# One attentional factorization kernel: its head is rebuilt and the transposes of the next batch block move from round 6 to round 12

## The reference

```
V = emb_v[x]                                   # x: 32 x 2048 indices
VV = V[iu] * V[ju]                             # 496 pairs
hid = relu(einsum('pbk,kh->pbh', VV, at_w) + at_b)
score = einsum('pbh,ho->pbo', hid, at_h)
pooled = sum(VV * score, axis=0)
logit = pooled @ p + w0 + sum(w1[x], axis=0)
prob = sigmoid(logit)
```

## Time and profile before

| What | Value |
|---|---|
| median of 3 runs | 841.13 us |
| span of the profiled execution | 835.8 us |
| runs' median less the span | 5.3 us |
| PE busy | 784.1 us (94%) |
| DVE busy | 722.5 us (86%) |
| ACT busy | 640.7 us (77%) |
| POOL busy | 555.4 us (66%) |
| PE share of the chain that ended last | 86% |
| DMA queue q0 (the gathers) | 16896 packets, 17.07 MB |

### The profile page before, as it was taken

One profiled execution on the slowest core, in us unless ns is written; L12 is line 12 of the kernel. 1 busy time (PEld: TensorE's weight loads), 2 busy tenths in 40 slices (PEclk: granted clock), 3 DMA queues, 4 the chain that ended last, 5 costly groups with the idle time before them and its releaser, 6 DMA issues.

```text
span 835.8 us, 26345 instructions
## 1 busy us (share of the span) xinstructions
PE 784.1 (94%) x10550; PEld 277.6 (33%) x10550; DVE 722.5 (86%) x1221; ACT 640.7 (77%) x674; POOL 555.4 (66%) x537
## 2 busy tenths in 40 slices
PE   0488996999999999999999999999999999999998
PEld 0123332333333333333333333333333333333332
DVE  4278897699999999999999999999999999999894
ACT  0267775788798887878878788898888888888785
POOL 5577777666677676666766766677667666766720
PEclk9989998999999999999999999999999999999999
DMA  7533268445423466544332347644434457633200
GB/s 257 99 25 24 26 22 25 23 22 22 23 22 23 20 22 23 21 22 24 21 22 22 23 21 22 23 24 21 22 21 23 21 22 23 24 22 22 11 1 1
DMA packets 19398, 24.27 MB, mean 29 GB/s; under 512 B 9960, under 2 KB 10029, under 8 KB 19373
## 3 DMA queue, kind: packets, MB, share of 16 engines
q0 software_dynamic: 16896, 17.07, 43.4%
q1 hardware_dynamic: 1535, 6.64, 2.1%
q10 hardware_dynamic: 942, 0.22, 0.1%
HBM read 20.59 MB, written 3.31 MB: 29 GB/s over the span
## 4 chain that ended last, share of the span: by engine, by line
PE 86%; DMA 5%; POOL 5%; issue 2%; ACT 1%; DVE 0%; ACTq 0%; POOLq 0%
PE Z L591 52%; PE SG L607 26%; POOL rows L303 5%; PE SG L621 4%; PE Z L553 4%; DMA rows<-table,joint_idx 3%; DMA rows<-in_L_rec_emb_v_dram,idx 2%; ACT pV L471 0%; ACT H L526 0%; DMA idx_raw<-in_r_x_dram 0%; PE Z L685 0%; ACT V L460 0%; PE Z L664 0%; ACT y_sb L537 0%; ACTq L247 0%
## 5 line engine op out<-in xcount | busy, mean ns | idle before, releaser
L303 POOL DMA_INDIRECT rows<-table,joint_idx x496 | 518.8, 1046 | 224.0 <-issue 139.7
L445 DVE TENSOR_TENSOR X<-V 128x992 f32<-128x992 f32 (+15 forms) x1024 | 635.6, 692 | 28.8 <-ACT V L500 14.8
L526 ACT ACTIVATE H<-Z,bias 128x1024 f32<-128x1024 f32 x512 | 529.7, 1121 | 113.2 <-PE Z L591 109.8
L591 PE MATMUL Z<-X,w_sb 64*64 64x512 f32 x4096 | 477.2, 600 | 7.4 <-DVE X L445 3.4
L591 PEld LDWEIGHTS Z<-X,w_sb 64*64 64x64 f32 x4096 | 147.0, 132 | 288.7 <-issue 283.2
L607 PE MATMUL SG<-H,score_w 128*32 128x512 f32 x2048 | 239.4, 597 | 0.0
L607 PEld LDWEIGHTS SG<-H,score_w 128*32 128x32 f32 x2048 | 56.8, 109 | 172.8 <-issue 96.0
L471 ACT ACTIVATE pV<-V,pmask 128x1024 f32<-128x1024 f32 x64 | 81.5, 1276 | 0.1
L413 DVE TENSOR_TENSOR prod<-SG,gram 128x512 f32<-128x512 f32 x32 | 22.1, 691 | 63.3 <-PE SG L607 63.3
L460 ACT COPY V<-Z 128x1024 f32<-128x1024 f32 x31 | 31.4, 1013 | 42.4 <-PE Z L553 42.4
L621 PEld LDWEIGHTS SG<-V,pV 128*32 128x32 f32 x4096 | 42.7, 109 | 23.9 <-issue 19.3
(11 more groups left out here) (46 smaller groups left out, 35.1 us busy)
## 6 DMA issues: line engine op xcount, KB each, us to landing
rows<-table,joint_idx POOLq DMA_INDIRECT x496, 3.7
table<-joined SPq DMA_DIRECT2D x4, 792.0 KB
H<-in_L_rec_emb_v_dram SPq DMA_DIRECT2D x4, 768.0 KB, 8.3
rows<-in_L_rec_emb_v_dram,idx POOLq DMA_INDIRECT x16, 5.3
w_all<-in_L_rec_w_dram,idx POOLq DMA_INDIRECT x16
idx_raw<-in_r_x_dram SPq DMA_DIRECT2D x2, 64.0 KB, 2.1
idx_raw<-in_r_x_dram ACTq DMA_DIRECT2D x2, 64.0 KB, 2.3
table<-tail SPq DMA_DIRECT2D x1, 54.7 KB
```

Source lines behind the costliest of these rows:

```text
L303: pool.indirect_dma_start(out=rows[t % 2][:, g * FILL_M + m, half, c0:c1], out_offset=None, in_=source, in_offset=bass.IndirectOffsetOnAxi ...
L445: last_one = nc.vector.tensor_tensor(xo, vj, vi.unsqueeze(3).to_broadcast(shape), ALU.mult)
L526: nc.scalar.activation(H[:, s % H_SLOTS, :, COLS * g:COLS * g + COLS], Z[:, z_slot(t, r), :, :], ACT.Relu, bias=bias[:, 0:1]).then_inc(hid ...
L591: done = nc.tensor.matmul(Z[64 * par:64 * par + 64, z_slot(t, r), half, :], w_sb[k, :], X[k, s % X_SLOTS, par, COLS * g:COLS * g + COLS], ...
```

## The change

The head is written in another way, and the order within a fill changes:

- ACT makes the joined table in place of DVE, with the same eight copies.
- On ACT's queue the load of the tail of `w1` moves ahead of the weights; the loads of `bias`, `p`, `h` and `w0` move from ACT's to SP's queue, behind the loads of the table.
- Fills 0 and 1 are gathered from the given table; POOL's waits for the joined table stand ahead of fill 2. The separate `w1` gathers at the end become 32.
- The semaphores `rows_landed` and the waits on them are gone. The constant `IN_FLIGHT` is 4, and no line of the changed kernel reads it or `HELD_FILLS`.
- `V` of fill 0 is copied from PSUM by DVE in place of ACT, and the constants that need `p` and `h` are made by DVE behind round 1 of fill 0.
- The transposes for every fill from 2 on stand ahead of round 12, and the scaled copies on ACT ahead of rounds 14 and 15.
- The loop over fills starts at fill 1.

```diff
-TURN_BEFORE, LATE_TURN = 6, 12
-LATE_FILLS = (1, 2)
+TURN_BEFORE, SCALE_BEFORE = 12, (14, 15)
...
-PLAIN_FILLS = 1
+PLAIN_FILLS = 2
...
-LANES, IN_FLIGHT, HELD_FILLS = 4, 3, 4
+IN_FLIGHT, HELD_FILLS = 4, 4
...
             sp.dma_start(tail[:, :, 1:1 + EMB], last_rows(emb_v)).then_inc(tail_loaded, 16)
+            for half in range(2):
+                lo, hi = half * 64, half * 64 + 64
+                sp.dma_start(bias[lo:hi, :], at_b.rearrange("(h o) -> h o", o=1)).then_inc(bias_loaded, 16)
+                sp.dma_start(pcol[lo:hi, :], p).then_inc(p_loaded, 16)
+                sp.dma_start(hcol[lo:hi, :], at_h).then_inc(h_loaded, 16)
+            sp.dma_start(w0_sb[:, :], w0.to_broadcast([QUARTERS, 1])).then_inc(w0_loaded, 16)
...
-                            n = GATHERS * t + 2 * (FILL_M * g + m) + half
-                            if held and n >= IN_FLIGHT:
-                                pool.wait_ge(rows_landed[(n - IN_FLIGHT) % LANES], 16 * ((n - IN_FLIGHT) // LANES + 1))
...
             gather(0)
+            pool.wait_ge(idx_ready, 2)
+            gather(1)
             pool.wait_ge(idx_ready, 4)
             pool.wait_ge(table_stored, 16 * (PIECES + 1))
-            gather(1)
             pool.wait_ge(first_turned, 2)
             gather(2)
...
+            act.wait_ge(w1_loaded, 32)
+            for c in (0, 1 + EMB):
+                nc.scalar.copy(joined[:, :, c], raw_w1[:, :]).then_inc(w1_joined, 1)
+                nc.scalar.copy(tail[:, :, c], tail_w1[:, :]).then_inc(w1_joined, 1)
+            for k in range(PIECES):
+                act.wait_ge(raw_loaded[k], 16)
+                r0, r1 = k * PIECE, (k + 1) * PIECE
+                nc.scalar.copy(joined[:, r0:r1, 1:1 + EMB], raw[:, r0:r1, :]).then_inc(rows_joined[k], 1)
...
-                        late = turn_before(t) == LATE_TURN
-                        if r == turn_before(t):
+                        if r == TURN_BEFORE:
                             keep_v(t + 1, 1 - parity)
-                        if r == (14 if late else 12):
+                        if r == SCALE_BEFORE[0]:
                             keep_pv(t + 1, 1 - parity, 0)
                             keep_w1(t + 1, 1 - parity)
-                        if r == (15 if late else 14):
+                        if r == SCALE_BEFORE[1]:
                             keep_pv(t + 1, 1 - parity, 1)
...
-            products(1, 1, False, False)
-            products(2, 0, False, False)
-            products(3, 1, False, False, head)
-            with pe.Fori(3, FILLS - 2, 2) as t:
+            products(1, 1, False, False, head)
+            with pe.Fori(1, FILLS - 2, 2) as t:
```

More of the change, by code:

```diff
@@ L195, in afm_kernel @@
         w1_first = sem("w1_first")
-        rows_landed = [sem(f"rows_landed{lane}") for lane in range(LANES)]
+        first_gathered = [sem(f"first_gathered{g}") for g in range(2)]
         first_turned = sem("first_turned")
@@ L222, in over_fills @@
             fill(0, 0, True, False)
-            fill(1, 1, False, False)
-            fill(2, 0, False, False)
-            with eng.Fori(3, FILLS - 2, 2) as t:
+            with eng.Fori(1, FILLS - 2, 2) as t:
                 fill(t, 1, False, False)
@@ L230, in gathered @@
         def gathered(t, parity):
-            return 16 * GATHERS // 2 * (t - parity - HELD_FILLS + 2)
-        def landed(gathers):
-            return 16 * gathers // LANES
+            return 16 * GATHERS // 2 * (t - (1 if parity else 2) + 2)
         def piece(dram, k):
@@ L348, in _ @@
                                         ).then_inc(idx_ready, 1)
-            dve.wait_ge(w1_loaded, 32)
-            for c in (0, 1 + EMB):
-                nc.vector.tensor_copy(joined[:, :, c], raw_w1[:, :]).then_inc(w1_joined, 1)
-                nc.vector.tensor_copy(tail[:, :, c], tail_w1[:, :]).then_inc(w1_joined, 1)
-            for k in range(PIECES):
-                dve.wait_ge(raw_loaded[k], 16)
-                r0, r1 = k * PIECE, (k + 1) * PIECE
-                nc.vector.tensor_copy(joined[:, r0:r1, 1:1 + EMB], raw[:, r0:r1, :]).then_inc(rows_joined[k], 1)
             nc.vector.memset(score_w[:, :, :], 0.0).then_inc(score_w_cleared, 1)
@@ L426, in products @@
                     if first and r in (0, STEPS // 2):
+                        first_keep_v(g)
                         dve.wait_ge(first_v, g + 1)
+                    if first and r == 2:
+                        loaded_consts()
                     if r == 8:
@@ L542, in turn @@
             def turn(t, parity):
-                if isinstance(t, int) and t < HELD_FILLS:
-                    for lane in range(LANES):
-                        pe.wait_ge(rows_landed[lane], landed(GATHERS * (t + 1)))
-                    pe.nop(nofuse=True)
-                else:
-                    pe.wait_ge(rows_gathered[parity], gathered(t, parity))
+                pe.wait_ge(rows_gathered[parity], gathered(t, parity))
                 embs = rows[parity][:, :, :, :].rearrange("p t h k -> p t (h k)")
@@ L557, in first_turn @@
             def first_turn(g):
-                for lane in range(LANES):
-                    pe.wait_ge(rows_landed[lane], landed(GATHERS // 2 * (g + 1)))
-                pe.nop(nofuse=True)
+                pe.wait_ge(first_gathered[g], 16 * GATHERS // 2)
                 if g == 1:
@@ L580, in hidden @@
                 pe.wait_ge(x_ready, ROUNDS * t + r + 1)
-                if r == turn_before(t) + 2 and not first and not last:
+                if r == TURN_BEFORE + 2 and not first and not last:
                     pe.wait_ge(v_ready, t + 1)
                 elif not first or r >= Z_SLOTS:
-                    pe.wait_ge(hid_ready, ROUNDS * t + z_before(t, r) + 1)
+                    pe.wait_ge(hid_ready, ROUNDS * t + z_before(r) + 1)
                 pe.nop(nofuse=True)
@@ L634, in products @@
                 for r in rounds:
-                    if r == turn_before(t) and not first and not last:
-                        pe.wait_ge(hid_ready, ROUNDS * t + turn_before(t) - Z_SLOTS + 1)
+                    if r == TURN_BEFORE and not first and not last:
+                        pe.wait_ge(hid_ready, ROUNDS * t + TURN_BEFORE - Z_SLOTS + 1)
                         turn(t + 1, 1 - parity)
```

68 lines of the change are left out of this document (29 added, 39 removed).

## The result

| What | Before | After |
|---|---|---|
| median of 4 runs each | 839.81 us (837.4 to 841.59) | 852.0 us (850.7 to 852.45) |
| ratio after to before | | 1.0155, 95% interval 1.0118 to 1.0192 |
| span of the profiled execution | 835.8 us | 850.6 us |
| that execution's own time | 837.4 us | 852.45 us |

The account below looks back on a forecast made before the run. PE alone was taken to set the pace in the loop. The terms summed as 835.8 + 21.1 - 6.8 - 0.6 - 8.1 = 841.4 us of span, +5.3 = 846.7 us, with a range of 838 to 861.

Parts of the forecast that it names:

- the likeliest case: Whole kernel: the forecast of 846.7 us, slower, with its own range of 842.5 to 850 and chance 0.60.
- The wait in the loop: Fills 5 to 30: PE waits for ACT's `pV` ahead of the inner products; 24.93 us a fill, +21.1 us.
- The 0.66 us for long products: Inner products as long as in fill 2, left out of the loop; as a rival 17 us on top, chance 0.10.
- Fills 3 and 4: Late transposes find fill 4's rows there, so the 6.74 us stall goes: -6.8 us.
- The head, -8.1: Up to fill 1: 16th gather lands at 32 in place of 40.1, fill 1's transposes stand at 55.5; -8.1 us.
- Edits costed at nothing: Rest of the head, such as ACT's joins, DVE's constants and small loads on SP's queue: put at nothing.
- The constants on DVE: First half of fill 0: under 1.1 us, hidden by the wait for the second half of its gathers.
- ACT's joins: Head: four joins on ACT take about 6 us together against DVE's 3.55, put at no cost.
- The 32 `w1` gathers: End: 16 further gathers go out until about 821, PE wants them at about 830; no cost.
- The 5.3 us around the span: Whole kernel: runs' median lies 5.3 us above the span of 835.8, added to the predicted span.
- That of the port pair: Head: GpSimd can't write descriptors during DVE's join, so the 4.48 us gather's extra 3.5 us go with it.
- That of the turns, packet by packet: Head: a gather should lose little beside bulk traffic, second half of fill 0 at about 28; not followed.

Follow-up runs that it names:

- e1: Kernel before, old head kept, with the transposes of every fill ahead of round 12; 1182.36 us, ratio 1.037, on a slow chip.
- f2: Changed kernel with both scaled copies ahead of round 14, one relu fewer in ACT's chain; 846.48 us, ratio 1.0071 to the kernel before.
- f4: Kernel before, old head kept, with every fill's transposes ahead of round 12 and both scaled copies ahead of round 14; 847.48 us, ratio 1.0056.
- f1: Kernel before with the whole new head and its own order of rounds kept; 843.8 us, ratio 1.0014.
- f3: Changed kernel with gathers of fills 0 and 1 held to three in flight and small loads back on ACT's queue; 855.21 us, ratio 1.0152.
- g4: Changed kernel with the eight joining copies on DVE again; run once, 853.54 us, where the kernel before takes 837.65.

## Why the prediction was right, and where it was not

The direction, the mechanism and the range were right: 852.0 us lies in 838 to 861, though 2 us over the likeliest case's own 842.5 to 850. The size was not: 12.2 us slower against 5.6. By its steps:

*The wait in the loop.* Right. Predicted was a wait of about 0.6 us or more ended by `pV`, and a period of 24.93 us; the trace has 0.54 us in all 26 and 24.79. The size was 0.14 us a fill too large: I took ACT's chain at 6.7 + 0.18 us, and it is 6.75, with 1.27 us and not 1.30 for a scaled copy. From the transposes' start to the inner products it took 496.17 - 488.23 = 7.94 us where I had 8.03. Without the few fills whose products are long the periods are 24.79 and 24.10 us: 26 x 0.69 = 18.0 us, and three such fills in place of one make it 19.2. `e1`, `f2` and `f4` show the mechanism from both sides: the wait comes with the late order under the old head too, and goes with one relu. The 0.66 us for long products was left out of the loop for a reason that doesn't hold, so that it came out nearly right is luck. It is not a matter of straight code: fill 2 of before, with 2.10 us, has two gather issues of POOL that end during its products (those at 119.16 and 120.41), and the loop shows the same in `f2` and `f4`.

*Fills 3 and 4.* Right in kind, -8.1 where I had -6.8. What I left out stands in the windows of the kernel before:

```profile
134.00:136.00 2.00, 0.00 (x0) 0.00 (x0) 1.52 (x3) 0.00 (x0) 1.53 (x2) 0.50 0.81 22
136.00:138.00 2.00, 1.99 (x12) 1.66 (x16) 0.00 (x0) 0.00 (x0) 1.55 (x2) 0.50 0.91 28
138.00:140.00 2.00, 2.00 (x16) 0.74 (x20) 0.32 (x1) 1.26 (x2) 0.43 (x2) 0.71 0.76 22
```

The 6.74 us stall lowered the granted clock to 0.50, and the transposes and the six rounds behind it took 1.5 us more. A stall costs its own length and the slow stretch after it. The row was there to be read: 1.97 us for transposes that take 1.09 elsewhere.

*The head, -8.1.* This step failed; measured is +0.2. I let the 16th gather land at 32; it landed at 39. I had moved its issue forward, from 36 to 24.5 (it went out at 23.6), and added a landing time of another stretch of the trace. The landing time is what grew: 3.5 us with three in flight on free DMA engines, 15.4 with no hold beside the table's traffic. The changed head was bound by how fast gathers land and not by when they are issued; `f1` (ratio 1.0014), `f3` and `g4` show the second half within about 2 us of the same place in differently built heads. The first half did gain 6.7 us, which nothing could use.

*Edits costed at nothing.* The constants on DVE were hidden in the end, but with 5.4 us of waiting ahead of them: they stood behind small loads of which I had only asked whether they delay the stores. The stores waited for SP's blocked queue and shared the DMA engines with the gathers: the four pieces were stored by 58 us and the table's tail by 62, against 26 and 30 before, and fill 2's gathers began at 63.00 where I had them at 47.3. So fill 2's rows were late: 2.25 us of waiting at 88.67 and 1.6 us of slow clock behind it (the transposes 1.47 us instead of 1.09, the 32 matmuls after them 4.92 instead of 3.66). That is the +3.5 of fills 1 and 2. `f3` wins 3.4 us of it back in fill 1 and gives it up again before and behind.

*ACT's joins.* Right: 5.59 us, where I had 6. *The 32 `w1` gathers:* their cover held; no wait for them appears.

*The 5.3 us around the span.* Wrong. They compared a median with another execution's span. The execution that was profiled took 837.4 us, 1.6 above its span, and after it is 1.85. With 1.7 in their place my sum would have been 843.1, 8.9 us below the median, where 846.7 misses by 5.3; that the error of this term hid part of the others was luck. Between the spans the miss is 9.2 us: the head (8.3) and fills 1 and 2 (4.1), less the loop, which I had too dear (1.9), and fills 3 and 4, which gained more (1.3).

*The two rules.* That of the port pair: the trace agrees, and `g4` shows it by itself. That of the turns, packet by packet: my reading, that a gather loses little, was wrong (39 and not 28 us). In the changed kernel between 36 and 60 us:

```profile
q0 software_dynamic: 484, 0.48, 66.6%
q1 hardware_dynamic: 287, 1.50, 15.1%
```

Worked out over 16 engines and 24 us, a gather's packet takes 528 ns for 1 KB and a store's 202 ns for 5 KB. If the queues take turns by packet, the bulk transfer loses more than the gather. The rule itself (the Trainium skill, DMA: Bandwidth & Descriptors, section "Queues, rings and completion order") may hold; no run here tests it, and `g4`, whose four pieces were stored by 38 us with no hold, shows that more than turns decides.

*What stays open.* How a gather issue on POOL and a long block of 128 short matmuls on PE hang together, though they always come together; why the stores of the table end 20 us apart in two heads without a hold; and what makes PE's pauses in straight code as different as 0.2 and 10.6 us.

## What to carry to other kernels

Where an operation is moved later, count the chain of work that it starts on the next engine against what the first engine still has to do; here 6.75 us against 6.13, in every fill. Before moving issues earlier, look whether the transfers are bound by issue or by landing: if the landing time rises as fast as the issue moves, nothing arrives sooner. Where equal instructions take two different times in one loop, lay the other engines' rows beside both kinds. Price a PE stall with the slow clock behind it, and check a gain in straight code against the pauses that straight code brings.

## What the runs showed of the hardware

- A pause of PE of 4.3 or 6.7 us was followed by 3 to 5 us in which the granted clock was 0.50 at first; pause and slow stretch together cost 7.4 and 8.3 us.
- Indirect gathers of 128 rows of 64 or 65 numbers went out one every 1.3 to 1.5 us in most fills, and never closer than 1.24 us. From issue to landing one took 3.5 us with three in flight, 9.2 with no hold in fill 4, and 9.7 to 15.4 with no hold beside the table's traffic.
- A block of 128 short matmuls took 1.30 us, or 1.5 to 2.15 us when an indirect gather's issue on POOL ended well inside it, in the loop at a granted clock of 1.00 in both kinds; 316 blocks of ten traces show no exception.
- The issue of one small load on SP's queue took 12.18 us behind five loads of the table, where the next ones took 0.6 to 1.3.
- An indirect gather's issue on POOL took 3.65 us beside three DVE copies of 128x1536 fp32 and 0.94 beside the same copies on ACT.
- In straight code PE paused up to 10.61 us for nothing that the trace shows, with one packet of an instruction queue inside the pause.
